# A GNN layer on one core: TensorE's relation loads moved behind the gate chunks, aggregate rows fetched three units ahead, node units started two pair steps later

## The reference

```
h    = relu(layernorm(x))
S    = h[src]
msgs = relu(relu(S @ W_rel[r].T + b_rel[r]) @ W_rel[r].T + b_rel[r])     # r = relation of the edge
agg  = segment_sum(msgs, dst)
i, f, g, o = split(agg @ W_ih.T + b_ih + b_hh, 4)
c    = sigmoid(i) * tanh(g);  hn = sigmoid(o) * tanh(c)
out  = x + (relu(relu(hn @ W1.T + b1) @ W2.T + b2) @ W3.T + b3)
```

## Time and profile before

| what | value |
|---|---|
| time, median of 3 runs (lowest, highest) | 2441.94 us (2438.3, 2446.62) |
| profiled execution: its own time, its span | 2442.41 us, 2440.8 us |
| PE busy | 2137.6 us, 88% |
| DVE busy | 1795.0 us, 74% |
| ACT busy | 1632.9 us, 67% |
| POOL busy | 1188.1 us, 49% |
| mean granted TensorE clock | 0.949 |

### The profile page before, as it was taken

How to read it: one execution, slowest core, us unless ns; L and a number is a source line. 1 busy time by engine, 2 the same in 40 slices (tenths; PEclk the granted TensorE clock), 3 DMA queues, 4 the chain that set the end, 5 groups by cost and what they waited for, 6 DMA issues and landing times.

```text
span 2440.8 us, 51857 instructions
## 1 busy us (share of the span) xinstructions
PE 2137.6 (88%) x14224; PEld 1411.5 (58%) x14225; DVE 1795.0 (74%) x4311; ACT 1632.9 (67%) x3366; POOL 1188.1 (49%) x917
## 2 busy tenths in 40 slices
PE   6858677767999999999999999999999999899997
PEld 5747565644665666665666566566666666444543
DVE  7547555555877778777777877787887877688885
ACT  2447555546777777777777777777777777566663
POOL 0037777775555555555555555555555543200000
PEclk7569988889999999999999999999999999999998
DMA  9946555556788888888888888888888887878786
GB/s 388 425 144 101 93 96 96 95 107 121 132 158 162 165 163 161 156 152 156 164 166 161 159 152 153 160 165 164 160 158 151 161 155 141 184 174 185 192 186 142
DMA packets 400606, 396.90 MB, mean 163 GB/s; under 512 B 263738, under 2 KB 343158, under 8 KB 394360
## 3 DMA queue, kind: packets, MB, share of 16 engines
q0 software_dynamic: 91200, 157.34, 39.8%
q1 hardware_dynamic: 306788, 238.12, 37.4%
q10 hardware_dynamic: 2516, 0.14, 0.1%
HBM read 185.88 MB, written 156.97 MB: 140 GB/s over the span
## 4 chain that ended last, share of the span: by engine, by line
PE 63%; issue 13%; ACT 10%; DMA 5%; POOL 4%; DVE 1%; SPq 1%; another core or an unknown queue 1%; POOLq 0%; ACTq 0%; DVEq 0%
PE bank L1472 30%; PE bank L1419 8%; PE bank L1486 5%; PE bank L1455 4%; PE bank L1438 4%; PE bank L1401 4%; DMA agg<-summed,scatter_idx 3%; PE bank L1511 3%; POOL agg L667 2%; POOL xg L651 2%; DMA a_lo<-row_lo 2%; ACT count_tmp L739 2%; ACT summed L727 2%; ACT tcell L786 2%; PE bank L1311 2%
## 5 line engine op out<-in xcount | busy, mean ns | idle before, releaser
L667 POOL DMA_INDIRECT agg<-summed,scatter_idx x400 | 638.2, 1596 | 676.5 <-DVE scatter_idx L1147 507.7
L1472 PE MATMUL bank<-a_hi,ihT 128*128 128x512 f16 x2400 | 716.8, 380 | 19.7 <-DMA a_lo<-row_lo 19.2
L651 POOL DMA_INDIRECT xg<-in_x,src_ring x400 | 453.6, 1134 | 269.1 <-DMA src_ring<-src_slot 137.3
L1472 PE MATMUL bank<-a_lo,ihT 128*128 128x512 f16 x1200 | 456.3, 380 | 0.0
L1472 PEld LDWEIGHTS bank<-a_hi,ihT 128*128 128x128 f16 x2400 | 234.4, 98 | 233.3 <-issue 26.6
L1438 PE MATMUL bank<-relT,h_hi 128*128 x1600 | 320.5, 275 | 0.0
L1419 PE MATMUL bank<-s_hi,relT 128*128 128x256 f16 x1600 | 305.3, 287 | 0.0
L1401 PE MATMUL bank<-ident,xn 128*128 128x128 f32 x800 | 132.1, 290 | 190.2 <-ACT xn L760 97.2
L675 POOL DMA_DIRECT2D y<-in_x x100 | 133.8, 1347 | 297.0 <-DVE y L1205 275.7
L1073 DVE SCALAR_TENSOR_TENSOR s_lo<-bank,s_hi 128x512 f16<-128x512 f32 x200 | 137.8, 689 | 161.4 <-ACT s_hi L733 140.3
L733 ACT ACTIVATE s_hi<-bank 128x512 f16<-128x512 f32 x200 | 119.7, 598 | 195.5 <-PE bank L1401 157.2
(11 more groups left out here) (197 smaller groups left out, 4718.9 us busy)
## 6 DMA issues: line engine op xcount, KB each, us to landing
agg_in<-agg SPq DMA_DIRECT2D x100, 512.0 KB
y<-in_x POOLq DMA_DIRECT2D x100, 512.0 KB, 6.5
out<-y SPq DMA_DIRECT2D x100, 512.0 KB
agg<-zeros SPq DMA_DIRECT2D x24, 2112.0 KB, 15.8
dst_ring<-dst_rows SPq DMA_DIRECT2D x200, 128.0 KB
xg<-in_x,src_ring POOLq DMA_INDIRECT x400
agg<-summed,scatter_idx POOLq DMA_INDIRECT x400
src_ring<-src_slot SPq DMA_DIRECT2D x200, 1.0 KB
```

The costliest lines, as they stand in the source:

```text
L651: nc.gpsimd.indirect_dma_start(out=xg[:, k.slot(8), t, :], out_offset=None, in_=x[:, :], in_offset=bass.IndirectOffsetOnAxis(ap=src_ring[: ...
L667: nc.gpsimd.indirect_dma_start(out=agg[:, :], out_offset=bass.IndirectOffsetOnAxis(ap=scatter_idx[:, k.slot(8), t:t + 1], axis=0), in_=sum ...
L1472: last = nc.tensor.matmul(N_C[c % 2][:, 0:UNIT], lhs, rhs, start=i == 0, stop=i == len(todo) - 1)
```

## The change

On TensorE, `relations` moves from the head of a step to behind `turn_s`, and where units run, behind the step's first two gate chunks as well. In SP's steps the order and the place of the unit work change: both transposes of unit u+1 now stand in its even step, and the load of a unit's rows (now unit u+3) and the store of unit u-4 in its odd step. ACT makes `row_hi` of unit u+2 in the odd step. DVE's order is the same. N0 becomes 60, so all unit steps come two steps later against the pairs.

```
-N0 = NB + 4
+N0 = NB + 6
 # SP
-                if not at.odd:
-                    k = at.unit + 2     # load agg_in; then k = at.unit - 4: store y
                 k = at.unit + 1
-                    if not at.odd:      # turn row_hi
-                    else:               # turn row_lo
+                if k.within(UNITS) and not at.odd:   # turn row_hi, then row_lo
+                k = at.unit + 3
+                if k.within(UNITS) and at.odd:       # load agg_in
+                k = at.unit - 4
+                if k.within(UNITS) and at.odd:       # store y
 # ACT, both_step
-                if not half:
-                    high_rows(k + 1)
+                if half:
+                    high_rows(k + 2)
 # PE
             def edge_step(at):
+                turn_s(at)
                 rel_of = relations(at)
-                turn_s(at)
                 layer_h(at - 1, rel_of.get(1))
             def both_step(at):
                 k, half = at.unit, at.odd
-                rel_of = relations(at)
                 turn_s(at)
                 chunk(k, 3 * half)
                 chunk(k, 3 * half + 1)
+                rel_of = relations(at)
                 layer_h(at - 1, rel_of.get(1))
```

More of the change, by code:

```diff
@@ L573, in step @@
                                  ).then_inc(dst_loaded[k.slot(2)], 16)
-                if not at.odd:
-                    k = at.unit + 2
[L576 to L596, removed]
@@ L597, in step @@
-                k = at.unit + 1
-                if k.within(UNITS):
-                    if not at.odd:
[L600 to L607, removed]
-                    else:
[L609 to L613, removed]
+                k = at.unit + 1
@@ new lines, in step @@
+                if k.within(UNITS) and not at.odd:
+                    sp.wait_ge(row_hi_ready, k.n + 1)
+                    sp.sem_inc(row_hi_cleared, 1)
+                    wait_from(sp, chunk_done, (k.n - 1) * CHUNKS)
+                    sp.sem_inc(row_hi_cleared, 1)
+                    sp.dma_start_transpose(a_hi[:, k.slot(2), :, :, :].rearrange("p t h n -> p (t h) n"),
+                                           row_hi[:, k.slot(2), :, :].rearrange("p t d -> p (t d)")
+                                           ).then_inc(a_hi_turned[k.slot(2)], 16)
+                    sp.wait_ge(row_ready, k.n + 1)
+                    sp.sem_inc(row_cleared, 1)
+                    sp.dma_start_transpose(a_lo[:, k.slot(2), :, :, :].rearrange("p t h n -> p (t h) n"),
+                                           row_lo[:, k.slot(2), :, :].rearrange("p t d -> p (t d)")
+                                           ).then_inc(a_lo_turned[k.slot(2)], 16)
@@ new lines, in step @@
+                k = at.unit + 3
+                if k.within(UNITS) and at.odd:
+                    row = first_row(mybir.EngineType.SP, k)
+                    sp.wait_ge(scattered, 32 * min(QUARTER_PAIRS + 2 * k.n, PAIRS) if isinstance(k.n, int)
+                               else 32 * PAIRS if at.about >= PAIRS else (QUARTER_PAIRS + 2 * k.n) * 32)
+                    sp.sem_inc(units_cleared, 1)
+                    wait_from(sp, row_ready, k.n - 1)
+                    sp.sem_inc(units_cleared, 1)
+                    sp.dma_start(agg_in[0:UR, k.slot(2), :, :],
+                                 unit_view(agg, row)).then_inc(agg_loaded[k.slot(2)], 16)
@@ new lines, in step @@
+                k = at.unit - 4
+                if k.within(UNITS) and at.odd:
+                    row = first_row(mybir.EngineType.SP, k)
+                    sp.wait_ge(x_added[k.slot(Y_SLOTS)], 16 * (k.turn(Y_SLOTS) + 1))
+                    sp.sem_inc(units_cleared, 1)
+                    o = k - 1
+                    wait_from(sp, stored[o.slot(Y_SLOTS)], 16 * (o.turn(Y_SLOTS) + 1))
+                    sp.sem_inc(units_cleared, 1)
+                    sp.dma_start(unit_view(out, row),
+                                 y[0:UR, k.slot(Y_SLOTS), :, :]).then_inc(stored[k.slot(Y_SLOTS)], 16)
```

## The result

The changed kernel takes 2327.93 us (median of 4, 2326.91 to 2333.45) against 2443.64 us; the ratio is 0.9535, interval [0.9518, 0.9552]. That is 116 us less. 79 were forecast, and 2328 lies outside the range that was given. TensorE's lines are 3 lower in the changed kernel's rows than in those of before, except in r1, r2, r7 and r10, which are made from the kernel before.

A forecast was written before the change was run, and what follows sets the result against it. PE was taken to set the pace with pairs and units together, idling in an issue gap from the relation load. 2442.4 - 67 - 4.6 - 7 + 1 - 1 = 2363.8 us (2363 against the median); 8-in-10 range 2342 to 2402.

The forecast's parts named there:

- part 1: Even step with units, PE: relation load hidden behind two chunks, 10.02 us instead of 10.73, -0.71 us.
- part 5: Steps of pairs alone: load delays layer_h but stays hidden; +1 us at the start, -1 us for last pairs beside units.
- that rival: TensorE's sequencer: about 62 ns decoding per matmul and weight load, transposes some 0.2 us late, total near 2380 us; no chance given.
- Part 2: Odd step with ACT's row_hi: 9.91 us, -0.66 from 10.57; after a root 10.52 us, -0.05.
- The discount: Steps with pairs and units: gain taken as 0.48 us a step, not 0.53, leaving 0.05 for gaps that stay.
- part 3: Shift by two steps: unit 0's step starts at 561 to 562 us without its wait; -4.6 us, bounds 0 and -7.
- part 4: Units alone: most of the 11.5 us of waits for a_lo goes; -7 us, bounds 0 and -11.
- Rival (a): Load in steps with units: the gap moves half, 0.35 us stays behind the chunks; 2412 us, chance 0.12.
- (b): Steps with units: no gain, the gap moves whole or ACT or DVE take over; 2430 to 2442 us, chance 0.06.
- (c): Load behind the chunks waits for TensorE to run dry, stopping the array 0.83 to 1.49 us; 2494 us, chance 0.07.
- (d): DMA transfers collide in the odd step, 10 to 25 us given back; 2375 to 2390 us, chance 0.75 together with the forecast.
- 12 us for the other parts: Gain assumed for the change apart from the relations' move, subtracted in pricing the slower case at 2494 us.

The follow-up runs named there:

- r1: Kernel before with relations moved behind the two chunks in steps with units only: 2357.38 us, ratio 0.9651.
- r2: Kernel before with relations moved behind turn_s in steps of pairs alone only: 2438.08 us against 2442.12, ratio 0.9988.
- r7: Kernel before with relations read once ahead of the steps, so no loads in them (wrong relation for most pairs): 2356.32 us, ratio 0.9642.
- r10: Kernel before with N0 = NB + 6 alone, so units start two steps later: 2430.57 us against 2433.43, ratio 0.9990.
- r5: Changed kernel with relations behind the transposes and only the first chunk in steps with units: 2342.74 us, ratio 0.9584.
- r6: Changed kernel with relations straight behind the transposes, ahead of both chunks, in steps with units: 2448.27 us, ratio 1.0027.
- r4: Changed kernel with ACT's row_hi back in the even step, for unit k+1: 2315.07 us, ratio 0.9470.
- r3: Changed kernel with relations back at the head of both kinds of step: 2500.57 us, ratio 1.0232.
- r8: r3 with relations read once ahead of the steps, so no loads in them (wrong relation for most pairs): 2333.24 us, ratio 0.9547.
- r9: r3 with row_hi in the even step again, leaving SP's order and the shift against the kernel before: 2483.22 us, ratio 1.0206.

## Why the prediction was right and wrong

The forecast's direction and its mechanism hold, the mechanism in part by luck (part 1). What failed is the size of the sum. Its main term, 139 steps shorter by 0.48 us, measured 0.67 us a step: the root's odd step was priced at -0.05 us and came at -0.37, and 0.05 us a step was held back for gaps that didn't stay. Next to it stands part 5, priced at +1 us, where the stage was 7.7 us shorter in the profiles. I compare the working term by term against the profiled executions (2442.41 and 2326.91 us, 115.5 apart).

- **Part 1**, even step: -0.71 forecast, 9.98 instead of 10.73 is -0.75. Right. But the reason that I gave for the cover was too timid. I took the load's path at 0.83 us, supposing that sums are issued at PE's speed. The load's own record in the kernel before, in the step end of 1205.54, shows otherwise:
```profile
L1388 PEldq TENSOR_LOAD <-pair_rel x1: 530/530/530, 1205.5 to 1205.5; - x1
```
It starts with the first sum, 0.2 us behind the end of `summed`, so the sums' issue costs the sequencer next to nothing. The path was the 1.49 us bound (0.53 of it the load; the transposes follow 0.83 us behind its end), and the cover 3.0 us, not 1.3. In the changed kernel the load took 1.24 us, so by the same 0.83 us its path was about 2.1 us (an estimate): with a cover of 1.3 us some 0.8 us would have shown. Path and cover were both taken too small, and that the load came out hidden as forecast is luck to that extent. What the sequencer needs for the sums, transposes and two chunks together shows in the step from 1134.57, `summed` first, then the load:
```profile
1133.19 0.58 ACT L724 COPY summed<-bank 128x512 f32<-128x512 f32 x1
```
```profile
L1385 PEldq TENSOR_LOAD <-pair_rel x1: 992/992/992, 1134.6 to 1134.6; - x1
```
That is 22 matmuls with their weight loads in some 0.8 us, at most 0.04 us each. The Trainium skill, "TensorE: Matmul & The Clock Gate", "Step-by-step: what each phase is for", gives 62 ns for each matmul where the sequencer decodes it in ucode. This isn't borne out here: 22 of them would be 1.36 us, and PE's transposes came 0.11 us behind the last sum in every step shown of the changed kernel. (By the prediction's own 0.2 us a step that rival's time would have been 28 us above the forecast, near 2392 us, not 2380.)
- **Part 2**, odd step: -0.66 forecast, 9.86 instead of 10.57 is -0.71. Root's odd step: -0.05 forecast, 10.20 instead of 10.57 is -0.37. This is the worst sized step. std ended at 1.19 us, as forecast (1.20), but the 3.37 us that I carried over from std to `g_g` held idle time. In the kernel before `s_hi` waited for PE's transposes and started 0.09 us behind std's end, and `g_g` started at 1210.16, as the last matmul of its chunk ended (1210.13). Without these the stretch is 3.07 us, as ACT's rows of the changed kernel show (step from 1144.55; std, `s_hi`, `g_g`, `g_o`):
```profile
1145.44 0.30 ACT L744 ACTIVATE std<-mean_var,eps 128x8 f32<-128x8 f32 x1
1145.65 0.58 ACT L730 ACTIVATE s_hi<-bank 128x512 f16<-128x512 f32 x1
...
1148.13 0.68 ACT L777 ACTIVATE g_g<-bank,gate_b 128x512 f32<-128x512 f32 x1
...
1151.10 0.69 ACT L777 ACTIVATE g_o<-bank,gate_b 128x512 f32<-128x512 f32 x1
```
- **The discount** of 0.05 us a step for gaps that stay, and the loop's turn (0.38 us every eighth step, another 0.05): both went too. Together 0.67 us a step instead of 0.48: 139 steps gave -93 us where -67 was forecast. That is 26 of the missing 37 us; the earlier step 60 (part 3) makes about 7 and the shorter end (part 4) 2.
- **Part 3**: step 60 was forecast at 561 to 562 and came at 554.73; the stage of pairs alone was 7.7 us shorter, which I had priced at +1 (**part 5**). The 0.7 us of exposed load ahead of `layer_h` is there as forecast (39.8 us in 56 pieces) and POOL covers it; that the stage got shorter was not in any case of mine. r2 (-4 us) and r10 (-3 us) are not clear of zero, so no run shows what shortened it.
- **Part 4**: from step 199 to the end 380.3 us, where 379.6 + 11.1 less 8 = 382.7 was forecast. Right within 2.4 us, though `a_lo` still waits 4.7 us.
- **Rival (a)**, half a gap: r5 and r6 show the stall to be path less cover; with two chunks nothing stays. **(b)**: ACT does bound the odd step; PE waits 0.36 us for it in the one shown and 0.70 us behind a root, and without `row_hi` there the two are 0.16 and 0.50 us shorter (r4). This was in the sum. **(c)**, the load waits for a dry array: no; r1 is 85 us faster, and the load runs beside matmuls. **(d)**: the transfers do collide, but with the load; nothing shows on the gathers, as PE's only wait left in the stage is the one for `summed`.

A reading that the prediction missed altogether is that the parts don't add. The move alone gives -85, the rest alone +58, the two together -116: the rest is worth -31 once the load is hidden. My 12 us for the other parts assumed the load's price to be the same in either order of SP; r3, r8 and r9 show that this order doubles the load's time and takes the gap from 0.63 to 1.04 us a piece. And the move without SP's order leaves waits for `a_lo` (r1), which I had not looked for in the stage of both.

## What to carry to other kernels

A register load on an engine's sequencer belongs behind the longest run of work that doesn't need it, since it runs while the queue drains; price its stall as its path less the work queued ahead, and look for its own record in the trace, as its duration isn't constant (0.53 to 2.0 us here). When a chain is carried over to a new timetable, take the waits out of it first, then add it up again. Measure the order of DMAs and the place of a load alone and together: here one of the two alone would have been thrown away at +2.3%, and one piece of the whole, `row_hi` in the odd step, is better left out (r4).

## What the runs showed of the hardware

The load of two integers from SBUF takes 0.53 us at the least and, with SP's new order of DMA transposes and 512 KB loads and stores, 1.0 to 1.24 us in the median; up to 1.7 us in the changed kernel, with the DMA share of the stage at 0.90, and up to 2.0 us in r4 and r5. When the array has run dry, TensorE's next matmul starts 0.83 us after the load's end (median of r3 and of the kernel before). The Trainium skill, "DMA: Bandwidth & Descriptors", section "Latency and other measured facts", gives such a load a floor of about 600 ns; the quiet ones here are below it, at 0.53 to 0.54 us, and the measurement decides. What in the traffic lengthens it (the share, the queue, the kind of packets) is open: a share of 0.70 left one at 530 ns. TensorE's sequencer was ahead of the array by four transposes and twelve 512-column matmuls with their weight loads, 3.0 us of work. The queue of 64 in the Trainium skill, "TensorE: Matmul & The Clock Gate", section "Architectural detail: the array is 16x 32x32, not 1x 128x128", allows that.
